# Softmax row sums taken from the exponentials' accumulated output in a fused cross-attention and mixture-of-experts kernel

## What is computed

```python
q = (Q @ Wq.T + bq); k = (K @ Wk.T + bk); v = (V @ Wv.T + bv)      # 16 heads of 8
scores = einsum('bhqd,bhkd->bhqk', q, k) / sqrt(8)
scores = where(mask == 0, -inf, scores)
attn = softmax(scores, axis=-1)
out = einsum('bhqk,bhkd->bhqd', attn, v)          # then @ Wo.T + bo
x = x + tanh(g_xattn) * attention(layernorm(x), ctx)
x = x + tanh(g_ffn) * experts(layernorm(x))       # top 2 of 8, weights by softmax
```

## Time and profile before

| | us |
|---|---|
| median of 3 runs | 493.05 |
| the three runs | 492.95, 493.05, 496.19 |
| span of the profiled execution | 490.1 |
| PE busy | 405.2 |
| ACT busy | 284.5 |
| POOL busy | 272.4 |
| DVE busy | 269.1 |

### The profile page before, as it was taken

How to read it: one execution, slowest core, us unless ns; L and a number is a source line. 1 busy time by engine, 2 the same in 40 slices (tenths; PEclk the granted TensorE clock), 3 DMA queues, 4 the chain that set the end, 5 groups by cost and what they waited for, 6 DMA issues and landing times.

```text
span 490.1 us, 12349 instructions
## 1 busy us (share of the span) xinstructions
PE 405.2 (83%) x4299; PEld 327.6 (67%) x4299; DVE 269.1 (55%) x1010; ACT 284.5 (58%) x848; POOL 272.4 (56%) x297
## 2 busy tenths in 40 slices
PE   0779999999999999999998459959479999999900
PEld 0556667677767767676776348959378999999800
DVE  1345656786877868777689433414323332333257
ACT  1268778787878788787877513423133544444334
POOL 8535319169598595894936403766735344554500
PEclk9979999999999999999999869998869999999965
DMA  3999999620000000000000182654538577777269
GB/s 75 240 352 410 413 406 242 94 58 19 20 18 19 20 23 13 24 14 25 12 25 13 34 264 90 204 170 150 172 92 270 171 242 233 219 233 231 88 228 297
DMA packets 48154, 72.55 MB, mean 148 GB/s; under 512 B 8053, under 2 KB 32637, under 8 KB 48093
## 3 DMA queue, kind: packets, MB, share of 16 engines
q1 hardware_dynamic: 43549, 62.32, 41.7%
q0 software_dynamic: 4544, 9.45, 5.5%
HBM read 41.83 MB, written 34.66 MB: 156 GB/s over the span
## 4 chain that ended last, share of the span: by engine, by line
PE 73%; DVE 8%; issue 6%; DMA 4%; ACT 3%; SPq 2%; POOL 2%; another core or an unknown queue 1%; POOLq 0%; DVEq 0%; ACTq 0%
PE U L718 7%; PE S L740 7%; PE T L718 7%; PE O L740 7%; PE S L624 7%; PE O L654 6%; PE T L632 5%; PE S L614 5%; PE U L632 5%; PE O L664 5%; DVE orec L1087 2%; ACT P L819 2%; DMA yg<-res 2%; DVE PT L1081 1%; PE E L673 1%
## 5 line engine op out<-in xcount | busy, mean ns | idle before, releaser
L819 ACT ACTIVATE P<-S,nmax 128x120 f32<-128x120 f32 x512 | 135.2, 420 | 5.3 <-DVE nmax L1075 5.3
L975 POOL DMA_INDIRECT res<-yo,dpos x78 | 74.9, 960 | 87.0 <-DVE yo L1238 79.5
L1075 DVE TENSOR_REDUCE nmax<-S 128x4 f32<-128x480 f32 x128 | 75.2, 649 | 45.8 <-PE S L624 41.1
L964 POOL DMA_INDIRECT zs<-z,posu x64 | 63.8, 996 | 59.3 <-DVE posu L1154 37.8
L856 ACT ACTIVATE H<-U,wbuf 128x256 f32<-128x256 f32 x82 | 34.4, 471 | 60.3 <-PE U L718 42.1
L614 PE MATMUL S<-mb_r,I_r 128*128 128x480 f32 x128 | 64.7, 509 | 2.0 <-ACT P L819 1.9
L826 ACT COPY PT<-U 120x512 f32<-120x512 f32 x63 | 39.3, 623 | 37.8 <-PE U L632 36.5
L856 ACT ACTIVATE H<-T,wbuf 128x256 f32<-128x256 f32 x74 | 31.1, 471 | 48.3 <-PE T L718 33.7
L938 POOL TENSOR_SCALAR Kb<-Kt,hm 128x480 f32<-128x480 f32 x32 | 47.0, 1483 | 18.1 <-ACT Kt L840 17.9
L928 POOL TENSOR_SCALAR z<-X,mv,rstd 128x128 f32<-128x128 f32 x64 | 50.3, 793 | 2.7 <-POOL rstd L923 2.4
L718 PE MATMUL T<-zT,wbuf 128*128 128x256 f32 x148 | 40.6, 398 | 12.5 <-DVE zT L1232 7.2
(11 more groups left out here) (161 smaller groups left out, 651.4 us busy)
## 6 DMA issues: line engine op xcount, KB each, us to landing
wbuf<-wpk SPq DMA_DIRECT2D x39, 578.0 KB
zs<-zero SPq DMA_DIRECT2D x1, 17952.0 KB, 59.9
zin<-zs SPq DMA_DIRECT2D x39, 132.0 KB
yg<-res SPq DMA_DIRECT2D x16, 256.0 KB, 4.1
wpk<-in_w SPq DMA_DIRECT2D x1, 2048.0 KB
wpk<-in_w SPq DMA_DIRECT2D x8, 256.0 KB
out<-X SPq DMA_DIRECT2D x16, 128.0 KB, 3.6
ctx_sb<-in_ctx SPq DMA_DIRECT2D x1, 1440.0 KB, 16.6
```

The costliest lines, as they stand in the source:

```text
L819: ins = nc.scalar.activation(P[:, n % 4, j, :], a[:, j * LK:(j + 1) * LK], ACT.Exp, bias=nmax[:, n % 4, j:j + 1])
L964: nc.gpsimd.indirect_dma_start(out=zs, out_offset=bass.IndirectOffsetOnAxis(ap=posu[:, F, k, i:i + 1], axis=0), in_=z2[:, F % 2, i, :], in ...
L975: nc.gpsimd.indirect_dma_start(out=res, out_offset=bass.IndirectOffsetOnAxis(ap=dpos[:, n % NDP, h:h + 1], axis=0), in_=yo[:, n % NYO, h, ...
L1075: v.tensor_reduce(nmax[:, n % 4, :], Sb[n % NHG][:, 0:HG * LK].rearrange("p (j k) -> p j k", j=HG), AX_X, ALU.max, negate=True).then_inc(m ...
```

## The change

`sums` leaves PE's program and `oneV` is gone. Each exponential instruction gets a second output, `accum_out`, which is the sum of its 120 results per partition: one number per query and head, in `esums` (two buffers of 4 x 4 columns). `exps` waits in addition for `rsum_done`, so that a buffer of sums is not overwritten too early; `s_free` now also says that the sums are there.

DVE gets a new `sums(k - 1)` at the head of round k, ahead of `row_max`: it waits for the last exponentials of batch k - 1, takes the reciprocals of the 16 columns (`rsum`), waits for its own result, and copies them, each repeated 8 times, into `rwide` (128 x 128). PE gets `scales(k - 1)`, one transpose of `rwide` into the half of `Ob` where the sums stood, ahead of the matmuls of `values(k - 1)` and behind its waits, with a wait for `rwide` of its own. `unload` copies that half to `orec` where it took the reciprocal before, and multiplies as before. `pv_done` comes behind the values instead of behind the sums.

The PT copy of step 4k + 2 moves from ACT (behind the exponentials) to DVE (behind `copy_pt(4k)` and, at p = 0, `route` part 2; ahead of the statistics and of the search). `copied` now reads: odd steps by ACT, even steps by DVE. In the set-up of the constants POOL leaves five fills of `oneV` away and one wait.

```diff
         def copied(eng, n):
-            if n >= 0 and n % NHG:
-                eng.wait_ge(pt_act, (NHG - 1) * (n // NHG) + n % NHG)
-            elif n >= 0:
-                eng.wait_ge(pt_dve, n // NHG + 1)
+            if n >= 0:
+                eng.wait_ge(pt_act if n % 2 else pt_dve, n // 2 + 1)
@@ PE, values
                 pe.wait_ge(o_free, k + 1)
                 steps_read()
+                begun["batches"] = k + 1
+                scales(k)
                 for g in range(NHG):
                     for j in range(HG):
-                        mm(Ob[32 * j:32 * j + 32, 0:LQ], Vm[:, G % 2, i * HG + j, 32 * g:32 * g + 32],
-                           PT[:, (NHG * k + g) % NPT, j * LQ:(j + 1) * LQ],
-                           start=(g == 0), stop=(g == NHG - 1), tile_position=(0, 32 * j))
-
-            def sums(k):
-
-                steps_read()
-                begun["batches"] = k + 1
-                for g in range(NHG):
-                    for j in range(HG):
-                        last = mm(Ob[32 * j:32 * j + 32, LQ:2 * LQ], oneV[:, g, :],
+                        last = mm(Ob[32 * j:32 * j + 32, 0:LQ], Vm[:, G % 2, i * HG + j, 32 * g:32 * g + 32],
                                   PT[:, (NHG * k + g) % NPT, j * LQ:(j + 1) * LQ],
                                   start=(g == 0), stop=(g == NHG - 1), tile_position=(0, 32 * j))
                 last.then_inc(pv_done, 1)
+
+            def scales(k):
+
+                pe.wait_ge(rwide_done, k + 1)
+                mm(Ob[:, LQ:2 * LQ], rwide[:].rearrange("p j g d -> p (j g d)"), I[:], start=True, stop=True,
+                   is_transpose=True)
@@ PE, round_: sums(k - 1) left out behind values(k - 1)
@@ ACT
             def exps(n):
                 act.wait_ge(max_done, n + 1)
                 wait(act, t_ready, n - 3)
+                wait(act, rsum_done, n // NHG - 1)
                 a = Sb[n % NHG]
                 for j in range(HG):
                     ins = nc.scalar.activation(P[:, n % 4, j, :], a[:, j * LK:(j + 1) * LK], ACT.Exp,
-                                               bias=nmax[:, n % 4, j:j + 1])
+                                               bias=nmax[:, n % 4, j:j + 1],
+                                               accum_out=esums[:, n // NHG % 2, n % NHG, j:j + 1])
                 ins.then_inc(s_free, 1)
@@ ACT, round_
                     copy_pt(NHG * k + 1)
-                    copy_pt(NHG * k + 2)
@@ DVE
+            def sums(k):
+
+                dve.wait_ge(s_free, NHG * (k + 1))
+                v.reciprocal(rsum[:], esums[:, k % 2, :, :]).then_inc(rsum_done, 1)
+                dve.wait_ge(rsum_done, k + 1)
+                v.tensor_copy(rwide[:], rsum[:].rearrange("p g j -> p j g").unsqueeze(3).broadcast_to((128, HG, NHG, DK))
+                              ).then_inc(rwide_done, 1)
+
             def unload(k):
 
                 dve.wait_ge(pv_done, k + 1)
+                v.tensor_copy(orec[:], Ob[:, LQ:2 * LQ]).then_inc(orec_done, 1)
+                dve.wait_ge(orec_done, k + 1)
                 G, i = divmod(k, GB)
-                v.reciprocal(orec[:], Ob[:, LQ:2 * LQ]).then_inc(orec_done, 1)
-                dve.wait_ge(orec_done, k + 1)
@@ DVE, round_
+                if 0 <= k - 1 < B:
+                    sums(k - 1)
                 if k < B:
                     for g in range(NHG):
                         row_max(NHG * k + g)
...
                 step(ks[3:4])
+                if k < B:
+                    copy_pt(NHG * k + 2)
                 if p == 1 and G - 1 in LAST:
```

More of the change, by code:

```diff
@@ L301, in build @@
         Vm = sb("Vm", [LK, 2, GB * HG, NHG * (32 + DK)])
-        oneV = sb("oneV", [LK, NHG, 32])
         nmax = sb("nmax", [128, 4, HG])
@@ L305, in build @@
         PT = sb("PT", [LK, NPT, HG * LQ])
+        esums = sb("esums", [128, 2, NHG, HG])
+        rsum = sb("rsum", [128, NHG, HG])
+        rwide = sb("rwide", [128, HG, NHG, DK])
         orec = sb("orec", [128, LQ])
@@ L394, in build @@
         o_free = sem("o_free")
+        rsum_done = sem("rsum_done")
+        rwide_done = sem("rwide_done")
         orec_done = sem("orec_done")
@@ L767, in round_ @@
                     values(k - 1)
-                    sums(k - 1)
                 for g in range(NHG - 1):
@@ L1017, in _ @@
             nc.gpsimd.memset(z2[:, :, :, D:ZW], 0.0)
-            nc.gpsimd.memset(oneV[:], 0.0).then_inc(const_done, 1)
+            nc.gpsimd.memset(Vm[:], 0.0).then_inc(const_done, 1)
             pool.wait_ge(const_done, 1)
[L1020 to L1023, removed]
             for G in range(2):
@@ L1352, in _ @@
                                  it[:, 0:NE].unsqueeze(2).broadcast_to((128, NE, NE)), ALU.is_le))
-            dve.wait_ge(const_done, 2)
+            dve.wait_ge(const_done, 1)
             values_in(0)
```

## The result

The changed kernel takes 523.49 us, the median of 4 runs (522.62 to 526.41), against 493.49 us (492.95 to 496.19) for the kernel before in the same comparison: ratio 1.0572, 95% interval 1.0519 to 1.0624. It is slower by some 30 us. The ratios given here are those on record; they are not the quotients of the medians beside them (here 1.0608) and lie up to 0.4% from these. The prediction was 516.5 us, with a range from 498 to 542.

The account below looks back on a forecast made before the run. PE was taken to bound the attention rounds, the bound moving to ACT: 31 x 8.50 + 13 x 0.50 = 270.0 us against 244.5, +25.5, with the tail +23.5. Hence 493.05 + 23.5 = 516.5 us, range 498 to 542.

Parts of the forecast that it names:

- The chain's three parts: ACT chain of a round: 2.19 us from scores to exponentials, 5.83 for the exponentials, 0.48 to the next scores; 8.50 in all.
- a = 0.11 us: Price on ACT of writing the sum, per exponential, between ends 0 and 0.20; taken from two one-column tanh instructions.
- The clock: Rival: TensorE's clock falls as PE idles in the rounds, about 1.1 us a round, +34, 551 us; chance 0.08.
- hidden, with 0.1 us to spare: PT copy of step 4k + 2 on DVE: first maximum done near 10.6 us, wanted by ACT at 10.69; costs nothing.
- its wait for the reciprocals costs nothing: PE in the rounds: transposed reciprocals are there at 1.5 us, wanted 2.3 us into the round; wait costed at nothing.
- values should never wait for DVE's wide copy: Sign expected in the profile after: PE's values matmuls show no wait for DVE's copy of the repeated reciprocals.
- Together -2.0: Tail: experts' scatter 0.75 us sooner in round 31, about 1.25 us of sums off PE's path in round 32.
- The sum is nearly free: Rival: accumulated output costs ACT nothing, rounds -18.8 us, 472 us with the tail; chance 0.10.
- DVE takes the bound: Rival: statistics, search and sums run 0.3 us longer, 3 in 4 rounds lose that: +7, 523 us; chance 0.08.
- 540 to 558 us: Rival: the read does not overlap its exponential, price 0.16 to 0.20 us each on ACT; chance 0.13.

Follow-up runs that it names:

- e2: Kernel before with the exponentials' accumulated output added and never read, PE's sums and the copies unchanged: 515.56 us, ratio 1.0402.
- e5: Changed kernel without the accumulated output (sums constant 1) and with the PT copies of step 4k + 2 back on ACT: 482.74 us, ratio 0.9732.
- e7: Changed kernel with 32 products with a constant put back on PE as filler, their result overwritten: 523.46 us, ratio 1.0529.
- e8: Changed kernel with DVE's new sums behind the first of the four maxima instead of ahead of it: 517.82 us, ratio 1.0447.
- e3: Kernel before with only the PT copies of step 4k + 2 moved from ACT to DVE: 499.78 us, ratio 1.0074.
- e1: Changed kernel with only the accumulated output taken away, the array of sums holding the constant 1: 493.16 us, ratio 0.9926.
- e4: Changed kernel with the PT copies of step 4k + 2 back on ACT, accumulated output kept: 516.91 us, ratio 1.0446.

## Why the prediction was right, and where it was not

**The direction and the mechanism.** The bound moved from PE to ACT as predicted, with one read for each exponential. The chain's three parts were 2.19 + 5.83 + 0.48; they measured 2.20 + 5.60 + 0.56 in round 17. The rounds predicted at 8.50, 9.00, 9.00 and 8.50 were 8.36, 8.89, 8.76 and 8.58; their sum is 34.59 against 35.0. e2 shows that the reads alone do it, e5 that without them the kernel would be faster.

**The read price.** The term was a = 0.11 us, the distance of two one-column tanh instructions. The exponentials' distance went from 0.248 to 0.337 or less, so a = 0.09. The estimate from the Trainium skill's ScalarE: Activation LUTs, "What ACT_TABLE_LOAD costs", was 93 ns, and the trace agrees with that estimate: 0.337 - 0.248 = 0.089 us. The page itself gives no time of a read. The read's own length, 253 ns in the mean, hardly matters, as it runs beside the next exponential. This mis-sized term alone would have made the rounds 31 x 8.25 + 13 x 0.50 = 262.3 us instead of 270.0.

**What made up for it.** 272.35 us were measured. The 10 us between come from things which the sum had at nothing or as a rival:

- The clock, 4.7 us in five rounds (above). As a rival it was to fall for good and cost 34 us; it fell here and there. e7 kept it up and gained nothing by it.
- DVE late at p = 0: 0.31 us in six rounds, 1.9 us. The step that failed is "hidden, with 0.1 us to spare" for the PT copy of step 4k + 2. The prediction did name the maxima as what is late next; e8 confirms it by taking 0.3 us out of those rounds. e3 shows that the copy costs 0.7% even without the reads, and e1 against e5 that it costs 6.1 us of the rounds where ACT is no longer slow.
- Round 30, 9.57 instead of 8.25 us: 1.3 us. The prediction took it for a round like the others. On DVE stand there, behind the copy, the table of the experts' rows and the statistics, as the timeline of DVE and then ACT shows:

```profile
289.42 0.28 DVE L1053 BATCH_NORM_AGGREGATE mv<-stat 128x2 f32<-128x6 f32 x3
...
290.01 2.34 DVE L1071 TENSOR_REDUCE nmax<-S 128x4 f32<-128x480 f32 x4
...
290.69 0.36 ACT L819 ACTIVATE P<-S,nmax 128x120 f32<-128x120 f32 x1 [1.21 <-DVE nmax L1071]
```

- An entry between the last exponential and the last mask: the key projection (182.46 in the timeline of PE above) at p = 1 and the query projection at p = 2. The rounds are 0.10 and 0.14 us longer than 8.25 and 8.75, seven of each, together 1.7 us. The 0.48 us behind the exponentials had been read where nothing was in the way.
- Rounds 0 and 7, 0.2 us longer than their place gives; in round 7 the maxima are late as well.

Together 4.7 + 1.9 + 1.3 + 1.7 + 0.4 = 10.0 us, and 262.3 + 10.0 = 272.3. The rounds had been forecast at 270.0: that they came within 2.4 us is luck, because a price of the read that was 7.7 us too high over the rounds nearly made up for 10.0 us that were left out. On the span, 522.0 us against the forecast 513.6, the larger part of the miss is the tail's, 5.9 us.

**PE.** That its wait for the reciprocals costs nothing holds in the rounds; "values should never wait for DVE's wide copy" does not. It waited four times, 4.4 us in all, and the two in the tail matter. Timeline of the tail, DVE, PE and POOL:

```profile
299.42 0.23 DVE L1084 COPY rwide<-rsum 128x128 f32<-128x128 f32 x1
299.79 0.30 PE L666 MATMUL O<-I,rwide 128*128 128x128 f32 x1 [0.92 <-DVE rwide L1084]
...
301.41 0.96 POOL L964 DMA_INDIRECT zs<-z,posu  x1 [4.44 <-PE O L658]
...
316.71 0.23 DVE L1084 COPY rwide<-rsum 128x128 f32<-128x128 f32 x1
317.08 0.45 PE L666 MATMUL O<-I,rwide 128*128 128x128 f32 x1 [1.56 <-DVE rwide L1084]
```

**The tail.** The sum gave -2.0 us: 0.75 for a scatter that comes sooner, 1.25 for sums that leave PE's path in round 32. Both are gone by these waits. The scatter starts 301.41 - 296.76 = 4.65 us behind the scores, as before (4.64), and in round 32 PE waits 1.56 us for the wide copy, where its sums had taken 1.60. So the step "Together -2.0" failed by 2.0 us through these waits. Why the tail is 3.9 us longer and not just as long stays open. The first product of the experts starts 22.6 us behind the scores of round 31, as in the kernel before (22.7), and PE ends 199.4 us behind them instead of 196.3, so most of the loss arises in the experts' part, which the change doesn't touch. From 80 to 100 us behind those scores PE was busy for 15.65 us at a granted clock of 0.58, against 11.91 us at 0.74 before; that would fit, and no run isolates it. The tail was between 221.5 and 225.4 us in e2, e4, e5 and e8, and 229.5 in e1, though these hold much the same work.

**The rivals.** "The sum is nearly free" gave 472 us from PE's chain and ACT's. With the reads out, e1 measured 493 and e5 483 us. In e1 DVE is late at p = 0, which that rival had left out. In e5 it is on time there, but the rounds at p = 1 and 2 take 7.72 and 7.80 us, not 7.61 and 7.35: their scores start 1.38 and 0.98 us behind the last exponential, where it is 0.54 at p = 0, so PE comes last there. Why PE needs more there than that rival gave it was not taken apart. "DVE takes the bound" gave 523 us, near what came, but by its own mechanism it explains only 3.2 us. The read does overlap, so 540 to 558 us was out.

**What beats both.** No kernel here that does the whole computation is faster than the one before. e5, whose row sums cost nothing, shows the room in this order of work: 2.7% for whoever gets them without an instruction on ACT.

## What to carry to other kernels

A by-product that looks free is to be priced on the engine that produces it: 0.09 us for each of 512 exponentials cost more than 32 matmuls a round gave back, since ACT's chain lay at most 1.55 us behind PE's and got 1.46 us longer. Before moving work to a third engine because it has idle time, follow what stands behind it up to the next thing that somebody waits for; DVE was idle for a quarter of the time, and one copy of 0.69 us a round in the wrong place cost 3.8 us of the rounds in e3 and 6.1 in e1. An experiment that undoes the two halves of a change separately and together shows what each hides from the other.

## What the runs showed of the hardware

The wide copy on DVE, 128 x 128 from SBUF to SBUF, is 0.23 us long in most rounds, but much longer beside some of POOL's work. Timeline of the changed kernel: a copy without such a neighbour (POOL works on 128 x 4 there), then one beside POOL's multiplication of the keys:

```profile
184.73 0.23 DVE L1084 COPY rwide<-rsum 128x128 f32<-128x128 f32 x1
...
191.87 2.96 POOL L938 TENSOR_SCALAR Kb<-Kt,hm 128x480 f32<-128x480 f32 x2
...
193.56 0.70 DVE L1084 COPY rwide<-rsum 128x128 f32<-128x128 f32 x1
```

Over the 32 copies it is 226 ns at least, 227 in the median and 751 at most. The six beside L938 take 0.42 to 0.75 us, one of the three beside POOL's L928 takes 0.43, and all others 0.23. The PT copies, which read PSUM, keep to 0.69 us. VectorE: DVE Perf Modes of the Trainium skill, "Two Vector instructions with no wait between them", speaks of a second SBUF read interface which Vector's 2-port mode shares with GpSimd; that would fit, and no run here tells it apart from other causes.

A reciprocal of 128 x 128 from PSUM took 0.96 us on DVE in the kernel before, and the copy that replaces it 0.28; the one of 128 x 16 takes 0.25. The new sums thus cost DVE no more in a round than the smaller `unload` gives back (0.25 + 0.23 against 0.68). What loaded it was the moved copy.
